# A fused transformer kernel: value projections lead the second attention block, and the first expert's products move into its last half

## The reference

```
1. attention, 16 heads of 128, weights = codes * block scales
2. MLP with ternary weights, silu(gate) * up, down
3. causal attention, 16 heads of 16:
     qkv = x @ w_attn + b_attn; att = softmax(mask(q k^T / 4)); y = att v
     out = y @ w_proj + b_proj
4. mixture of experts, 16 experts of 128 and a shared one of 256:
     w, idx = top_k(sigmoid(h @ gate_w.T), 8);  w = 2.5 * w / (sum(w) + 1e-6)
     out = shared(h) + sum_e comb[:, e] * (silu(h Wg_e) * (h Wu_e)) Wd_e
```

## Time and profile before

| | us |
|---|---|
| median of 3 runs | 2279.35 |
| lowest, highest | 2278.01, 2289.25 |
| the profiled execution's own time | 2277.4 |
| its span, first to last instruction | 2275.7 |
| second attention block, from | 1513.3 |
| first down product of the experts | 1935.02 |

### The profile page before, as it was taken

The page is one execution under the profiler, slowest core; times in us unless marked ns, Lnnn a source line. Parts: engine busy times, 40 slices in busy tenths (PEclk is TensorE's granted clock), DMA queues, the critical chain, the costliest instruction groups (busy, mean ns, idle before and its releaser), DMA issues. The chain is left out here.

```text
span 2275.7 us, 35924 instructions
## 1 busy us (share of the span) xinstructions
PE 2124.8 (93%) x12680; PEld 1710.0 (75%) x12680; DVE 1471.2 (65%) x2614; ACT 1184.2 (52%) x2158; POOL 573.9 (25%) x558
## 2 busy tenths in 40 slices
PE   4999999999999999999999989978899889899996
PEld 3888888888888888888888877754555445788885
DVE  4766776676676676676667774547676772655555
ACT  3654554565465465455556555426665665433333
POOL 3012012031031031031021105313333343544443
PEclk8999999999999999999999998988899897999998
DMA  2010010010010010010020002000000001010001
GB/s 80 1 40 2 1 40 2 1 40 2 1 40 2 1 40 2 1 40 2 1 40 29 8 2 72 1 8 3 3 6 4 1 1 49 29 42 22 21 1 37
DMA packets 37686, 41.02 MB, mean 18 GB/s; under 512 B 7936, under 2 KB 33408, under 8 KB 37504
## 3 DMA queue, kind: packets, MB, share of 16 engines
q1 hardware_dynamic: 37504, 38.57, 6.3%
HBM read 36.45 MB, written 2.10 MB: 17 GB/s over the span
## 5 line engine op out<-in xcount | busy, mean ns | idle before, releaser
L735 ACT ACTIVATE attn_probT_hi<-psum 128x512 fp32r<-128x512 f32 x512 | 278.3, 595 | 305.0 <-PE psum L621 305.0
L777 DVE TENSOR_REDUCE attn_neg_max<-psum 128x1 f32<-128x1024 f32 x256 | 313.3, 1224 | 179.8 <-PE psum L81 179.0
L823 DVE TENSOR_TENSOR attn_probT_lo<-psum,attn_probT_hi 128x512 fp32r<-128x512 f32 x512 | 327.6, 682 | 37.6 <-ACT attn_probT_hi L735 37.5
L714 ACT ACTIVATE attn_prob<-psum,attn_neg_max 128x1024 f32<-128x1024 f32 x256 | 286.8, 1120 | 7.0 <-DVE attn_neg_max L777 7.0
L621 PE MATMUL psum<-ident_sb,attn_prob 128*128 128x128 f32 x2048 | 267.0, 273 | 20.6 <-ACT attn_prob L714 11.4
L621 PEld LDWEIGHTS psum<-ident_sb,attn_prob 128*128 128x128 f32 x2048 | 237.3, 140 | 61.4 <-DVE attn_probT_lo L823 13.3
L552 POOL TENSOR_TENSOR attn_v_lo<-x_sb,attn_v_hi 128x512 fp32r<-128x512 f32 x64 | 82.0, 1281 | 766.8 <-ACT attn_v_hi L743 766.8
L2101 ACT ACTIVATE attn_probT<-psum 128x512 f32<-128x512 f32 (+3 forms) x384 | 165.2, 493 | 100.0 <-PE psum L1986 95.0
L81 PE MATMUL psum<-attn_probT_hi,attn_v_hi 128*128 128x512 f32 x512 | 212.5, 415 | 0.6 <-DVE attn_probT_lo L823 0.6
L81 PE MATMUL psum<-attn_probT_lo,attn_v_hi 128*128 128x512 f32 x512 | 201.3, 393 | 0.0
L81 PE MATMUL psum<-attn_key_hi,attn_q_hi 128*128 128x512 f32 x512 | 200.9, 392 | 0.2 <-DVE attn_key_lo L809 0.2
(11 more groups left out here) (209 smaller groups left out, 4882.7 us busy)
## 6 DMA issues: line engine op xcount, KB each, us to landing
attn_v_all<-in_moe_w SPq DMA_DIRECT2D x23, 384.0 KB, 3.0
acc_sb<-in_x SPq DMA_DIRECT2D x4, 512.0 KB, 5.7
x_sb<-in_wq_codes SPq DMA_DIRECT2D x8, 256.0 KB, 2.5
x_sb<-in_wq_scales SPq DMA_DIRECT2D x32, 64.0 KB, 3.0
x_sb<-in_wk_codes SPq DMA_DIRECT2D x8, 256.0 KB, 3.9
x_sb<-in_wk_scales SPq DMA_DIRECT2D x32, 64.0 KB, 4.9
x_sb<-in_wv_codes SPq DMA_DIRECT2D x8, 256.0 KB, 5.4
x_sb<-in_wv_scales SPq DMA_DIRECT2D x32, 64.0 KB, 5.8
```

The source lines that it names most:

```text
L714: nc.scalar.activation(prob[:, i % 2, :], scores(i).rearrange("p a b -> p (a b)"), ACT.Exp, bias=neg_max[:, i % 2:i % 2 + 1], accum_out=to ...
L735: nc.scalar.activation(probT[0][:, g % 2, half_tile * GT:(half_tile + 1) * GT, j * P:(j + 1) * P], ring(use).rearrange("p (t n) -> p t n", ...
L777: nc.vector.tensor_reduce(neg_max[:, i % 2:i % 2 + 1], scores(i), AX.XY, ALU.max, negate=True).then_inc(max_ready, 1)
L823: nc.vector.tensor_tensor(to[1], ring(use).rearrange("p (t n) -> p t n", n=P), f32(to[0]), ALU.subtract).then_inc(ring_free, 1)
```

## The change

The maxima of unit 5 move out of layer 2's block and open layer 3's (FIRST = 6). The four value jobs of batch 0 move from steps -4 and -3 to -6, -6, -5, -4, and value jobs come first among a step's jobs. A step's value and project jobs stand ahead of PE's second pair of maxima, other jobs at the end. DVE waits for the constants in `take_v` and no longer at its start. `copy_o` stands ahead of the first exponential. For the experts: the logits go two tiles to a step at 88 to 91, the weights are split at 84 and 89, `gate_up(0)` comes at 86, SiLU of p = 0 at 94 and product, hi and lo of p = 0 at 95; SiLU becomes a function of its own.

```diff
-    LEAD, AHEAD, FIRST = 11, 2, 5
+    LEAD, AHEAD, FIRST = 11, 2, 6
-    V_FIRST = (-4, -4, -3, -3)
+    V_FIRST = (-6, -6, -5, -4)
-    ROUTER_AT, LOGITS_AT, SIGMOID_AT, BEST_AT, WEIGH_AT = 78, range(TOTAL - LEAD + 1, TOTAL - LEAD + 9), TOTAL - 2, TOTAL - 2, TOTAL - 1
-    LOAD_IN, SPLIT_AT, BEGIN_AT = HALVES - 1, (TOTAL - 6, TOTAL - 5), TOTAL - 2
+    ROUTER_AT, LOGITS_AT, SIGMOID_AT, BEST_AT, WEIGH_AT = 78, range(TOTAL - 8, TOTAL - 4), TOTAL - 2, TOTAL - 2, TOTAL - 1
+    LOAD_IN, SPLIT_AT, BEGIN_AT = HALVES - 1, (TOTAL - 12, TOTAL - 7), TOTAL - 10
-        23: ([("max", 4, 1)], [("max", 5, 0), ("max", 5, 1)]),
+        23: ([("max", 4, 1)], []),
...
-        found += [("v", 0, 0, n) for n, at in enumerate(V_FIRST) if at == g]
+        found = [("v", 0, 0, n) for n, at in enumerate(V_FIRST) if at == g] + found
         if g in V_AT:
-            found.append(("v", BATCH - 1, 0, V_AT.index(g)))
+            found = [("v", BATCH - 1, 0, V_AT.index(g))] + found
...
+    IN_FRONT = ("v", "project")
...
-                if g == TOTAL:
+                if g == TOTAL - 1:
                     moe.hidden_lo(pool, 0)
...
-            def small(g):
+            def small(g, in_front):
                 for n, (kind, of, c, part) in enumerate(jobs(g)):
+                    if (kind in IN_FRONT) != in_front:
+                        continue
...
-                    if projects and pair == pairs - 1:
-                        small(g)
+                    if pair == pairs - 1:
+                        small(g, True)
...
-                if not projects:
-                    small(g)
+                small(g, False)
                 if g in LOGITS_AT:
-                    t = LOGITS_AT.index(g)
-                    if t == 0:
-                        pe.wait_ge(max_free, HALVES * HALF_FILLS)
+                    n = LOGITS_AT.index(g)
+                    if n == 0:
...
-                    mm = moe.logits(pe, (t,), MAX_BANKS - 1)
+                    mm = moe.logits(pe, (2 * n, 2 * n + 1), MAX_BANKS - 1)
...
                 if g == BEGIN_AT:
+                    pe.wait_ge(max_free, HALVES * HALF_FILLS)
                     moe.gate_up(pe, 0)
...
-                    if h == 2 and r == quad_start[1] and 0 <= half < HALVES:
+                    if h == 0 and r == quad_start[1] and 0 <= half < HALVES:
                         copy_o(half, 0)
-                    if h == 2 and r == 0 and 0 < half <= HALVES:
+                    if h == 0 and r == 0 and 0 < half <= HALVES:
                         copy_o(half - 1, 1)
...
-                if g == TOTAL:
+                if g == TOTAL - 2:
                     act.wait_ge(weighed, (HALVES - 1) * QUADS)
+                    moe.silu(act, 0)
+                if g == TOTAL - 1:
                     act.wait_ge(stacked, HALVES * chunks * 2 * pairs)
                     moe.hidden_hi(act, 0)
...
                 t = b * ST + 2 * n
+                dve.wait_ge(consts, 128)
                 dve.wait_ge(misc_full, use + 1)
...
+                if g == TOTAL - 1:
+                    moe.product(dve, 0)
                 if g == BEST_AT:
...
                     if g == TOTAL:
-                        moe.product(dve, 0)
                         wait_misc_read(dve, last_outs["out", HALVES - 1, 0, 1])
...
-            dve.wait_ge(consts, 128)
             for i in range(2):
```

More of the change, by code:

```diff
@@ L1266, in split_hi, with silu @@
         self.nc.scalar.activation(self.half_of(0, v, slice(0, self.cols)), self.staged[v % self.STAGED], ACT.Copy).then_inc(self.w_hi_done, 1)
-    def hidden_hi(self, act, p):
+    def silu(self, act, p):
         act.wait_ge(self.gate_full, p + 1)
@@ L1272, in hidden_hi @@
         self.nc.scalar.activation(self.gate_act[p % 2], self.k.psum[:, self.slots[p % 2][0], :], ACT.Silu).then_inc(self.silu_done, 1)
+    def hidden_hi(self, act, p):
         act.wait_ge(self.prod_done, p + 1)
@@ L1286, in scalar @@
         if p + 1 < len(self.steps):
+            self.silu(act, p + 1)
             self.hidden_hi(act, p + 1)
@@ L2055, in step @@
                 weigh_behind = 1 if quads[g % QUADS][1] == 0 else 0
-                projects = any(job[0] == "project" for job in jobs(g))
                 for pair in range(pairs):
@@ L2065, in step @@
                         weigh_v(g)
-                if not projects:
-                    small(g)
+                small(g, False)
                 if g in LOGITS_AT:
-                    t = LOGITS_AT.index(g)
-                    if t == 0:
-                        pe.wait_ge(max_free, HALVES * HALF_FILLS)
+                    n = LOGITS_AT.index(g)
+                    if n == 0:
                         pe.wait_ge(moe.r_ready, 1)
                         pe.wait_ge(after.lo_done, BATCH_GROUPS * KC)
-                    mm = moe.logits(pe, (t,), MAX_BANKS - 1)
-                    if t == len(LOGITS_AT) - 1:
+                    mm = moe.logits(pe, (2 * n, 2 * n + 1), MAX_BANKS - 1)
+                    if n == len(LOGITS_AT) - 1:
                         mm.then_inc(moe.logits_full, 1)
                 if g == BEGIN_AT:
+                    pe.wait_ge(max_free, HALVES * HALF_FILLS)
                     moe.gate_up(pe, 0)
```

## The result

| | before | after |
|---|---|---|
| median, us | 2281.56 (20 runs) | 2267.36 (20 runs) |
| lowest, highest | 2275.65, 2290.77 | 2259.5, 2278.54 |
| profiled execution: time, span | 2277.4, 2275.7 | 2262.12, 2260.4 |
| block start, first down product | 1513.36, 1935.02 | 1508.72, 1920.02 |

The ratio is 0.9944, interval [0.9927, 0.996]: 0.56% faster, about 12.8 us. The forecast was 2261.4 with a range of 2250 to 2274; the profiled executions differ by 15.3 us where 16.0 was forecast. Both profiled executions are faster than their kernel's median, by 4 and 5 us.

A forecast was written before the change was run, and what follows sets the result against it. No engine bounds a whole stage; with TensorE busy 93%, only its idle and low-clock time can be won. Against the profiled 2277.4 us, -5.8 - 5.2 - 2.5 - 2.5 = -16.0 gives 2261.4, range 2250 to 2274.

The forecast's parts named there:

- Part 1: Opening of the second attention block: earlier start and no VectorE wait for constants, -5.8 us, bounds -4.0 and -7.5.
- Part 2: Changes of query chunk: copying the output bank before the first two exponentials shortens PE's waits, -5.2 us, bounds 0 and -6.5.
- The sum -6.5: Attention halves: PE wait saved at nine chunk-change places, -6.5 us, before letting 80% of the 1.2 us steps last.
- the clock of the middle: Between 1536 and 1893.1: with less idle PE time some clock falls vanish, -2.5 us, bounds 0 and -10.
- the five falls: Middle: five stretches at half clock right at or after copy waits, 20.4 us together, counted as costing 10.2.
- keep the clock up: Rival, last half: gate and up products at step 86 keep the clock up, 2253 us; chance 0.14.
- Part 3: Last half of the heads into the experts: moved expert products and paired logits, -2.5 us, bounds +5 and -11.
- case (a): Last half: the clock falls in step 88 and stays low through the logits, +3 us; weight 0.45.
- (b): Last half: the clock falls at step 90 and comes back in step 93, -4.5 us; weight 0.35.
- The end swallows the gain: Rival, block's end: ScalarE's new queue order and low clock eat the gain, 2269 to 2274 us; chance 0.22.
- The boundary waits only change their name: Rival, chunk changes: the next scores wait for exponentials or VectorE's maxima instead, 2269.1 us; chance 0.10.
- Slower: Rival, step heads: `copy_o` waits for unfinished weighing, exponentials queue behind; decides from 1.8 us at each of 16 places; chance 0.04.

The follow-up runs named there:

- e1: The kernel before with `copy_o` moved ahead of the first exponential and nothing else; 2254.45 us, ratio 0.9902.
- e3: The kernel after with the whole last part (logits, splits, gate and up products) as before; 2254.18 us, ratio 0.9905.
- e12: The kernel after with the whole last part as before, run a second time; 2259.22 us, ratio 0.9923.
- e8: The kernel after with VectorE's wait for the constants back at its start; 2276.84 us, ratio 0.9983.
- e4: The kernel after with `copy_o` back behind the first two exponentials; 2273.81 us, ratio 0.9981.
- e9: The kernel after with single logits tiles at steps 86 to 93 and the last `copy_o` ahead of the first `hidden_hi`; 2254.43 us, ratio 0.9893.
- e10: The kernel after with the old last part, but weights split at 84 and 89 and `gate_up(0)` at 86; 2255.17 us, ratio 0.9901.
- e2: The kernel before with the opening's edits and the front place of values alone; 2268.85 us, ratio 0.9952.
- e6: The kernel after with the logits one tile a step at steps 86 to 93, as before; 2259.78 us, ratio 0.9918.
- e5: The kernel after with the last `copy_o` ahead of the first expert's `hidden_hi` in ScalarE's queue; 2260.53 us, ratio 0.9923.
- the repeat: The kernel after, unchanged, run a second time; 2271.7 us, ratio 0.9962.

## Why the prediction was right, and where it wasn't

**The number** was right, 2261.4 against a median of 2267.36 and a profiled 2262.12; the same kernel's second median, 2271.7, is still in the range but outside the forecast's own 2254 to 2268. It was right as a sum, and in part by luck: of the 15.3 us between the profiled executions 2.1 came ahead of the change, the middle gave 1.2 more than forecast and the last part 3.8 less.

**Part 1, the opening, -5.8: right in the trace, -5.4.** Block start 2.6 earlier by the maxima of unit 5, wait of 5.84 gone, first exponentials 5.4 earlier than upstream explains. The limit was the one named: key, table load, exponential. The table load is followed by the exponentials at once (1527.31 + 1.28, and 1528.60), and so are the sigmoid (1907.55, 1908.84) and the SiLU (1909.14, 1910.43). The Trainium skill (ScalarE: Activation LUTs, What ACT_TABLE_LOAD costs) adds some 1.38 us of drain to each switch; none of these three rows shows it. What I hadn't foreseen is that the gain isn't additive. Beside the old last part and copy first it isn't there at all in the times (e1 against e3 and e12): the lead of some 5.6 us at the second projection (from the end of the first MLP's last copy) is some 2.8 at the third to fifth and gone by the ninth, where the kernel with the new opening (e3) is at 1.2 GHz in stretches (1649.1 to 1652.6, 1696.9 to 1700.3, and a third later, 1765.2 to 1768.6) that e1 lacks. On the kernel before, the opening alone is worth 11 us, twice its term. In the change itself the constants' wait is worth 9 us (e8). Why the clock falls at other places when the opening is shorter stays open.

**Part 2, `copy_o` ahead of the exponentials, -5.2: the step that was mis-sized.** The mechanism was right: waits of 11.1 us became 2.3, and little took their place (PE's waits for `attn_probT` in the middle grew from 6.1 to 8.0 us, those for the maxima shrank from 19.4 to 18.2). The sum -6.5 is what the waits gave in the change itself, 8.8 to 2.3 between e4 and after; it left out the ninth place, step 88. The middle gave 8.9 where this term and the clock of the middle (-2.5) made 7.7. What failed is the assumption that a wait is worth its length and at most a part of the five falls next to it. Copy first alone is worth 22 us, 8.3 of it waits; the rest goes with 51 us less at 1.2 GHz, 24 in the middle and 27 in the last half. The forecast had looked for the latter only as an effect of the products at step 86, the rival *keep the clock up*. Its time came true, by another edit, in e1, e3, e9 and e10; in the change as made it didn't. That moving the copy cuts the time at 1.2 GHz is shown, by the traces and by the clock of all executions (e1 against before, 119 and 173 us). That the wait of step 88 does it is not shown: in the kernel before and in e2 the clock had fallen 0.4 us before that wait began. What in the earlier course decides the fall stays open.

**Part 3, the last half, -2.5: wrong in sign.** In the trace the part from step 86 on lost 1.3 against before. Against the old last part with copy first it loses 8 to 13 us in the medians (2267.36 and 2271.7, against 2254.18 and 2259.22), and by the ratios some 9 both times. Two steps of the forecast were borne out: the clock falls in step 88 as in case (a) and comes back after 27.3 us, between (a) and (b); PE waits 4.22 us for the last copy, forecast 4.3, with a second fall of 3.4 us behind it. What was missing is the comparison: I measured this part against a last half at 1.2 GHz, which part 2 had already mended. Pairing the logits brings the low clock back, the late copy brings the wait. For the pairs as the cause of the long stretch speak the traces: four of the five with pairs have one stretch of 27.3 us, and the six with single logits and copy first have at most 7 us at 1.2 GHz ahead of the eighth group. The times alone settle it less: e6 against after, and e9 against e5 (2254.43 and 2260.53), have overlapping intervals. The fifth trace with pairs (e8) fell in four pieces instead of one long stretch, so what the pairs change is how likely and how long a fall is, not a fixed number.

**The clock of the middle, -2.5.** Before, ten stretches were at 1.2 GHz between 1536 and 1893.1; after, there were five from the opening's end on, but one of them is 20 us long (1530 to 1550). The five falls that the forecast named are all gone, after and in e1, where it let a quarter of their cost go; together the ten make 47.8 us, the five 41.0. The sign was right, and a us at 1.2 GHz costs nearer 0.3 us than the half that was counted; the size in the change can't be separated from part 2.

**The rivals.** *The end swallows the gain* describes the last part well (pairs and late copy). Of the 2269 to 2274 that it gives the first median, 2267.36, stays 1.6 short, as the middle gave more; the second, 2271.7, lies inside, so it isn't excluded by the times. *The boundary waits only change their name* is refuted by the waits and by e4: with the copy back 2273.81, PE waits for `attn_o` in its weighing 8.8 us again. *Slower*: no copy at the head of its step waited for PE; at 1742.07 it follows the key at once.

## What to carry to other kernels

When a change has several parts, price each one against the kernel that the others leave, not against the kernel before: a stretch at low clock that one edit mends can't be mended again, but it can be brought back. Waits of one microsecond can cost more than their length: here 8.3 us of them went with 22 us. Look at the granted clock of the whole stretch, in all executions and not in one profile, and look at whether a fall begins before or behind the wait that you blame. Before work is drawn into an engine's queue ahead of a copy that the bottleneck needs, write down the queue and put the copy first.

## What the runs showed of the hardware that was not expected

- Recorded busy time alone neither kept the clock up nor brought it back. In the kernel after it fell at 1881.20, with PE recorded busy 8.53 of the 8.53 us before. Then PE was recorded busy 27.30 of 27.30 us at 1.2 GHz through the paired logits and what lies between them (27.00 of 27.00 in the repeat, 27.50 of 27.50 in e5). The Trainium skill (TensorE: Matmul & The Clock Gate, What's actually happening) says that activity releases the throttle; by the recorded busy share these traces don't show that here, while in e6 the clock came back 7 us after a fall at the first single logits.
- The clock can be lost and regained in the same kernel at different places from one execution to the next: the kernel after ran from 2259.5 to 2278.54, and the two copies of one kernel, e3 and e12, both had 7 us at low clock in the last half but 4 us difference to the first down product; e12 was at 1.2 GHz for one stretch of 27 us in the middle (1764.5 to 1791.8), where e3 had two of 3.4 and 6.8. With such a scatter differences under about 5 us between two of these kernels aren't settled.
